# Indirect transfers over 128 partitions instead of 125 in a four-layer graph network kernel

## The reference

```python
x = _layernorm(x + _L0_gnn_ref(x, edge_attr_16, src, dst, W1, W2, attn, bias))   # attention, softmax per dst
x = _layernorm(x + _L1_gnn_ref(x, edge_index, edge_weight, ...))                 # attention, two norms, MLP 64-128-64
x = _layernorm(x + _L2_gnn_ref(x, edge_index, W, b))                             # h = segment_sum(x[dst]*norm, src) @ W.T + b
x = _layernorm(x + _L3_gnn_ref(x, src, dst, edge_weight, 100000))                # segment_sum(value * x[dst], src)
```

## Time and profile before

| | |
|---|---|
| runs | 3195.58 us median of 3 (3189.33 to 3202.84) |
| span of the profiled execution | 3201.0 us (the profile gives no other time of that execution) |
| PE, DVE, ACT, POOL busy | 66%, 50%, 50%, 65% of the span |
| queue 0 | 83200 packets, 47.29 MB |
| queue 1 | 164998 packets, 154.80 MB |
| mean granted TensorE clock | 0.806 |

### The profile page before, as it was taken

The page is one execution under the profiler, slowest core; times in us unless marked ns, Lnnn a source line. Parts: engine busy times, 40 slices in busy tenths (PEclk is TensorE's granted clock), DMA queues, the critical chain, the costliest instruction groups (busy, mean ns, idle before and its releaser), DMA issues. The chain is left out here.

```text
span 3201.0 us, 28668 instructions
## 1 busy us (share of the span) xinstructions
PE 2113.5 (66%) x9124; PEld 1064.1 (33%) x9124; DVE 1605.6 (50%) x3036; ACT 1614.0 (50%) x2303; POOL 2069.5 (65%) x1609
## 2 busy tenths in 40 slices
PE   5887587779888888999998664588888800012220
PEld 3433243336533333744443543233333200011120
DVE  4875588874887777344444177543334300012321
ACT  3776366653577787377777242376667700001110
POOL 6888888810078880057775888868881068888887
PEclk9999788887988999799999675688999955555555
DMA  2222122213522221134446543221111101112221
GB/s 55 64 67 64 39 64 49 48 38 94 186 45 47 44 44 45 41 95 119 119 109 148 110 115 97 60 49 42 39 45 55 36 15 14 14 40 58 58 57 26
DMA packets 251595, 204.25 MB, mean 64 GB/s; under 512 B 182627, under 2 KB 192167, under 8 KB 251446
## 3 DMA queue, kind: packets, MB, share of 16 engines
q1 hardware_dynamic: 164998, 154.80, 17.1%
q0 software_dynamic: 83200, 47.29, 9.0%
q10 hardware_dynamic: 3248, 0.34, 0.1%
HBM read 133.83 MB, written 79.64 MB: 67 GB/s over the span
## 5 line engine op out<-in xcount | busy, mean ns | idle before, releaser
L854 PE MATMUL ps<-wk 127*64 127x125 f32 x1200 | 120.1, 365 | 567.6 <-DVE wk L839 566.5
L2216 POOL DMA_INDIRECT stab<-wk,rank_i x200 | 251.4, 1257 | 272.6 <-issue 247.5
L509 ACT ACTIVATE b_s<-ps,vec 128x512 f32<-128x512 f32 (+1 forms) x444 | 296.2, 682 | 127.5 <-PE ps L506 74.7
L2213 POOL DMA_INDIRECT u<-x2tab,dpos_i x200 | 279.5, 1398 | 80.4 <-issue 78.6
L2213 POOL DMA_INDIRECT u<-in_x_dram,dst_i x200 | 267.8, 1339 | 61.0 <-issue 58.5
L2213 POOL DMA_INDIRECT u<-x3tab,src_i x200 | 258.3, 1292 | 72.5 <-issue 72.2
L2213 POOL DMA_INDIRECT u<-in_x_dram,src_i x200 | 250.3, 1252 | 73.7 <-issue 70.0
L854 PEld LDWEIGHTS ps<-wk 127*64 127x64 f32 x1200 | 95.5, 190 | 590.5 <-DVE wk L839 585.5
L884 ACT ACTIVATE e_a<-ps 128x500 f32<-128x500 f32 x75 | 43.9, 585 | 439.6 <-PE ps L854 439.0
L2213 POOL DMA_INDIRECT e_b<-x0tab,dpos_i x72 | 91.7, 1274 | 250.5 <-issue 250.5
L494 PE MATMUL ps<-b_h,blk_c 128*128 128x512 f32 (+1 forms) x296 | 177.9, 686 | 74.4 <-ACT b_gl L517 71.1
(11 more groups left out here) (415 smaller groups left out, 5547.5 us busy)
## 6 DMA issues: line engine op xcount, KB each, us to landing
b_gl<-in_x_dram SPq DMA_DIRECT2D x98, 256.0 KB
out_dram<-b_gl SPq DMA_DIRECT2D x98, 256.0 KB
wk<-dlist SPq DMA_DIRECT2D x50, 500.0 KB
wk<-slist SPq DMA_DIRECT2D x50, 500.0 KB
u<-stab SPq DMA_DIRECT2D x25, 510.0 KB
x2none<-b_gl SPq DMA_DIRECT2D x25, 250.0 KB
wk<-x2none SPq DMA_DIRECT2D x25, 240.0 KB
x2tab<-wk SPq DMA_DIRECT2D x25, 240.0 KB
```

The source lines that it names most:

```text
L509: return nc.scalar.activation(b_s[l][:, 0:w], pB[l][:, 0:w], ACT.Abs_reciprocal_sqrt, bias=col(EPSV))
L854: last_a = nc.tensor.matmul(e0[64 * (k % 2):64 * (k % 2) + 64, P * (k // 2):P * (k // 2) + P], msg[n % 2][0:P + 2, D * k:D * k + D], sr[n ...
L2213: pool.indirect_dma_start(out=o, out_offset=None, in_=tab, in_offset=at(ix), **kw).then_inc(s, 16)
L2216: pool.indirect_dma_start(out=tab, out_offset=at(ix), in_=a, in_offset=None, bounds_check=rows_n - 1, oob_is_err=False).then_inc(s, 16)
```

## The change

Every indirect transfer has 128 partitions on both sides. The five index tiles get 128 partitions. Partitions 125 to 127 of the gathers' indices are 0, so that they fetch row 0 of the table into three partitions that nobody reads (for gathers D the index of those partitions is that of `dpos_i`, which is `dps_i`; for gathers E `src_i`, which is `spos_i`). For the scatters they hold `SKIP`, above the bound, and are left out. The memsets of partitions 96 to 128 of these tiles stand at the start of DVE's list, and one, of `fidx_i`, with a wait of its own in `l2w_dve`. The copies that fill the index tiles name their 125 partitions. The group loops, the waits, the number of transfers (1,600) and `P` stay.

```diff
-        src_i, dst_i, dpos_i, rank_i, sfin_i = (sb(n, [P, TC], i32) for n in ("src_i", "dst_i", "dpos_i", "rank_i", "sfin_i"))
+        src_i, dst_i, dpos_i, rank_i, sfin_i = (sb(n, [128, TC], i32) for n in ("src_i", "dst_i", "dpos_i", "rank_i", "sfin_i"))
...
-                nc.vector.tensor_copy(dst_i[:, :], e0[0:P, 0:TC]).then_inc(S("dst_ready"), 1)
+                nc.vector.tensor_copy(dst_i[0:P, :], e0[0:P, 0:TC]).then_inc(S("dst_ready"), 1)
...
-            nc.vector.tensor_copy(spos_i[:, :], rmisc[0:P, :, 2])
-            nc.vector.tensor_copy(fidx_i[:, :], rmisc[0:P, :, 3]).then_inc(S("s_index"), 1)
+            dve.wait_ge(S("dve_step"), stepped(nc.vector.memset(fidx_i[96:128, :], int(SKIP))))
+            nc.vector.tensor_copy(spos_i[0:P, :], rmisc[0:P, :, 2])
+            nc.vector.tensor_copy(fidx_i[0:P, :], rmisc[0:P, :, 3]).then_inc(S("s_index"), 1)
...
-                    gather(xs[0:P, b, :], x, src_i[:, b:b + 1], gathered(0, g)[0])
+                    gather(xs[:, b, :], x, src_i[:, b:b + 1], gathered(0, g)[0])
...
-                    gather(xd[0:P, b, :], x, dst_i[:, b:b + 1], gathered(1, g)[0])
+                    gather(xd[:, b, :], x, dst_i[:, b:b + 1], gathered(1, g)[0])
...
-                    gather(ring[g % 3][0:P, D * k:D * k + D], x0tab, dpos_i[:, GC * g + k:GC * g + k + 1], ringed(g)[0])
+                    gather(ring[g % 3][:, D * k:D * k + D], x0tab, dpos_i[:, GC * g + k:GC * g + k + 1], ringed(g)[0])
...
-                    scatter(stab, E, rank_i[:, GC * g + k:GC * g + k + 1], rec[g % 2][0:P, RW * k:RW * k + RW], S(f"placed{g % 2}"))
+                    scatter(stab, E, rank_i[:, GC * g + k:GC * g + k + 1], rec[g % 2][:, RW * k:RW * k + RW], S(f"placed{g % 2}"))
...
-                    gather(rsrc[0:P, b, :], x2tab, dps_i[:, b:b + 1], gathered(2, g)[0], E)
+                    gather(rsrc[:, b, :], x2tab, dps_i[:, b:b + 1], gathered(2, g)[0], E)
...
-                    gather(rdst[0:P, b, :], x3tab, spos_i[:, b:b + 1], gathered(3, g)[0], E)
+                    gather(rdst[:, b, :], x3tab, spos_i[:, b:b + 1], gathered(3, g)[0], E)
...
-                    scatter(out, N, ix[:, b:b + 1], ring[(NG + n) % 3][0:P, D * k:D * k + D], ringed(NG + n)[0])
+                    scatter(out, N, ix[:, b:b + 1], ring[(NG + n) % 3][:, D * k:D * k + D], ringed(NG + n)[0])
...
             nc.vector.memset(w_e[:, :, :], 0.0)
+            nc.vector.memset(wk[96:128, 6144:], 0.0)
+            for a in (src_i, dst_i, dpos_i):
+                nc.vector.memset(a[96:128, :], 0)
+            for a in (rank_i, sfin_i):
+                nc.vector.memset(a[96:128, :], int(SKIP))
             dve.drain().then_inc(S("cleared"), 1)
```

More of the change, by code:

```diff
@@ L2004, in prep2_dve @@
             if k == 0:
-                nc.vector.tensor_copy(dpos_i[:, :], e0[0:P, 0:TC])
-                nc.vector.tensor_copy(rank_i[:, :], e0[0:P, TC:2 * TC]).then_inc(S("e0_free"), 1)
+                nc.vector.tensor_copy(dpos_i[0:P, :], e0[0:P, 0:TC])
+                nc.vector.tensor_copy(rank_i[0:P, :], e0[0:P, TC:2 * TC]).then_inc(S("e0_free"), 1)
                 nc.vector.tensor_copy(disd[:, :], e1[0:P, 0:TC])
@@ L2009, in prep2_dve @@
             else:
-                nc.vector.tensor_copy(dps_i[:, :], e0[0:P, 0:TC])
+                nc.vector.tensor_copy(dps_i[0:P, :], e0[0:P, 0:TC])
                 nc.vector.tensor_copy(diss[:, :], e0[0:P, TC:2 * TC]).then_inc(S("e0_free"), 1)
@@ L2015, in prep2_dve @@
             dve.wait_ge(S("prep2_ps"), 2 * k + 2)
-            nc.vector.tensor_copy((fidx_f, sfin_i)[k][:, :], e0[0:P, 0:TC]).then_inc(S("e0_free"), 1)
+            nc.vector.tensor_copy((fidx_f, sfin_i)[k][0:P, :], e0[0:P, 0:TC]).then_inc(S("e0_free"), 1)
             dve.drain().then_inc(S("prep2_done"), 1)
@@ L2052, in srcix_dve @@
             dve.wait_ge(S("src_ps"), 1)
-            nc.vector.tensor_copy(src_i[:, :], e1[0:P, 0:TC]).then_inc(S("src_ready"), 1)
+            nc.vector.tensor_copy(src_i[0:P, :], e1[0:P, 0:TC]).then_inc(S("src_ready"), 1)
             nc.vector.tensor_copy(ew[:, :], e1[0:P, TC:2 * TC]).then_inc(S("e1_free"), 1)
```

## The result

2926.86 us median against 3193.06 us, ratio 0.9163 with an interval of [0.9147, 0.9179]: 266 us faster. 3018 us had been forecast, in a range of 2880 to 3210.

What follows compares the result with a forecast made beforehand. POOL's back-to-back transfers were taken to bound F alone and A, B and D partly, with C and E hidden. F -80, A -40, B -28, D -32 and memsets +2 made -178 us: 3018 us median, range 2880 to 3210.

Steps and rivals of the forecast that it cites:

- no change: Rival, whole kernel: making up a transfer is fixed work or rows stay on few engines; +2 us, 3198 us, chance 0.14.
- The layout: Indirect transfers: 125 rows lie on five engines, 25 each; 128 rows would lie on 16, 8 each, 32 packets a transfer.
- POOL's time for one transfer: Every indirect transfer on POOL: -0.20 us each, between bounds of -0.78 and +0.03; issue time of 0.30 us stays.
- F: Last phase, 400 scatters, where POOL alone works: 400 x 0.20 = -80 us, all on the path.
- A: First phase, 400 gathers: 80 us of POOL time, only DVE's 56.3 us of waiting can go; 40 us gained.
- B: Second phase, 200 gathers into the ring: 40 us offered, 33.2 waited for by DVE; 28 us gained.
- D: Fourth phase, 200 gathers with a bound: 40 us offered, 40.9 waited for by DVE; 32 us gained.
- E: Fifth phase, 200 gathers with a bound: 0 us, hidden by the dense blocks, as POOL then stands 157.1 us.
- C and the added memsets: Phase C's 200 scatters: 0 us, hidden by the records' pipeline; added memsets on DVE: +2 us (0 to +2.5).
- the other signs: Profile after: 12800 packets in F, F about 549 us, DVE's waits mostly gone, A's end earlier by less than 80 us.
- the large gain: Rival, whole kernel: 0.50 us less a transfer, all waits used up; -328 us, 2868 us, chance 0.12.
- Slower: Rival, every transfer: POOL pays per row, three more rows cost 0.03 us; +38 us, 3234 us, chance 0.18.

Runs made afterwards that it cites:

- the sweep: Changed kernel with 312 more transfers behind it, alone on the core, 13 row counts from 128 to 16; scatters 0.98 us at 128 rows, 1.19 at 125.
- 63 alone: Kernel before, with only phase A's first 400 gathers at 128 partitions: 3129.93 us, ratio 0.9794.
- 19 alone: Kernel before, with only phase B's 200 gathers into the ring at 128 partitions: 3172.88 us, ratio 0.9939.
- 49 alone: Kernel before, with only phase D's 200 gathers with a bound at 128 partitions: 3143.24 us, ratio 0.9838.
- 43 alone: Kernel before, with only phase E's 200 gathers with a bound at 128 partitions: 3149.34 us, ratio 0.9857.
- the kernel with F only: Kernel before, with only the 400 last scatters at 128 partitions and three memsets of ring tiles: 3100.45 us, ratio 0.9694.

## Why the prediction was right

The range of 2880 to 3210 us held the case of no change as well, so that the number fell into it says little. What counts is which of its terms hold.

**The layout: right.** 5 engines with 25 rows each before, 16 with 8 after: 32 packets a transfer, and 127, 126, 124 and 120 rows behave by the same division.

**POOL's time for one transfer: right in kind, too small.** I took -0.20 us between ends of -0.78 and +0.03, and it is -0.21 for a scatter and -0.27 for a gather. The part that the rows of before showed, the bound test, was no guide: in the sweep's medians it costs 0.045 us with 25 rows an engine and 0.053 with 8 (0.997 against 0.944), so it does not go by rounds. The rounds are in the rest. The -0.20 was a geometric middle of two ends, of which the smaller, 0.04 us, took the bound test to go by rounds: that it comes so near to 0.21 is luck. With 0.27 for the gathers the terms of A, B and D would have been DVE's whole waits, 56 + 33 + 41 us, and the sum would still have been 55 us short.

**F: right, 80 forecast, 89 to 95 measured.** 400 x 0.208 = 83 us (medians 1.190 and 0.982), and the stalls of single transfers shrank as well: the groups' busy time fell by 504.4 - 405.8 = 98.5 us. About 5 us of it are lost again at the end of the program, see below.

**A: 40 forecast, 63 alone.** The way to the number was to cap the gain at DVE's waits on those gathers, 56 us, and to take a share. The cap was nearly right: of 110 us only 52 to 63 come through.

**B: 28 forecast, 19 alone.** **D: 32 forecast, 49 alone** (44 to 59 by the interval, 45 by its stretch), a little above the cap of 40.9 us that DVE's waits seemed to set. POOL's list of D became 58 us shorter in the kernel with D alone, and 14 us of it came back in a longer stand before E (13 us between the last gather of D and the first of E before, 27 then). E's first gather follows the end of layer 2, so it is that end that counts and not the sum of one engine's waits.

**E: 0 forecast, 43 alone. This is the step that failed.** I held E hidden because POOL stands 157 us behind it. That wait says that POOL was early for F, not that nobody was late for E's gathers: PE's list has the products of E between the dense blocks, and F waits for the last dense block. The trace of before had the row (34.3 and 51.2 us of waits at L1296). I read DVE's waits and not PE's there. A sign in the prediction said it as well: POOL's standing before F was to grow beyond 157 us, and it was 154. Had E been hidden, it would have grown by about the 50 us that E's gathers got shorter.

**C and the added memsets: right**, 5 us by the starts of the phases where 0 was forecast, and about nothing where +2 was.

Of the other signs, 12800 packets in F, DVE's waits of the earlier trace rows gone (1.2 us left for the ring in B, none for gathers in A and D) and a scatter of 0.98 us came as said. A's last gather came 110 us earlier where less than 80 was said, F was 14 us shorter than the 549 said.

2927 us lies between the forecast case (3018) and the large gain (2868 us), and nearer to the latter. The sum of 178 us fell short by 88: 43 in E, 23 in A, 17 in D, 15 or less in F, less 9 in B.

**The rivals.** "No change" is excluded by 32 packets a transfer and by the ratio. "Slower", three rows more to pay for, is excluded by the sweep: 120 rows take as long as 128 and 125 take longer. The Trainium skill (DMA: Bandwidth & Descriptors, Anatomy of one DMA) calls descriptor generation small and says that many can be emitted before the incremental cost shows. That does not hold for indirect transfers here: POOL pays 12 ns for each row of an engine from 8 to 25, and no less between 6 and 8 rows (0.92 to 0.98 us). The Trainium skill's rule on how many engines share a transfer, the largest number up to 16 that divides the rows (DMA: Bandwidth & Descriptors, Why a DMA increments its semaphore by 16 and not by 1), is what the times and packets of all 13 sizes follow.

## What to carry to other kernels

Choose the number of rows of an indirect transfer by its largest divisor up to 16, so that many engines share it with few rows each, and not by what divides the data. Here 125 rows cost POOL 0.2 to 0.27 us more than 128, and 127 cost 1.6 us more. Filler rows that nobody reads or that the bound leaves out cost next to nothing: 120 and 128 rows lie 0.02 us apart, and a scatter with three rows left out takes the same 0.98 us as one with none. An engine that stands idle after a phase does not prove that the phase is hidden; look who else waits for that phase's data, on every engine with a fixed order. And an order planned for old costs need not get better when the costs are corrected: it has to be timed.

## What the runs showed that I had not expected

**A hot row.** Queue 0 in phase B, before (884 to 1201 us) and after (833 to 1110 us):

```profile
q0 software_dynamic: 9541, 6.58, 19.0%
```

```profile
q0 software_dynamic: 6313, 6.49, 66.7%
```

The share of the 16 DMA engines rose from 19.0% to 66.7%, 60 to 185 us of all 16, for as many bytes; B alone at 128 shows it too (66.8%). In A it went from 10.7% to 12.7%, which is 68 and 67 us of all 16, in F down from 10.5% to 6.6%. The gathers of B also land late: 5.3 us at the median into `e_c`, against 3.8 in the kernel with F only, whose B has 125 rows. B gathers from `x0tab`, where every source without incoming edges has the same row, the last. Many engines that read one address at a time would explain it; no run tested that with other indices. Nothing in the trace makes it the reason why B gave least: DVE's waits for the ring fell to 1.2 us in the changed kernel.

**The end of the program.** From the start of the last scatter to the end of the span it is 3201.0 - 3197.4 = 3.6 us before and 2928.9 - 2920.4 = 8.5 after, and 8.5 to 9.0 in each kernel with F at 128 partitions and nothing behind it, 3.6 to 3.7 in each with F at 125. In the changed kernel the last packet is through at 2922.2 us, and behind it the profile shows neither an instruction nor a packet. Some 5 us of the gain are lost there, for a cause that stays open.
